# Weighted sums over four streams in a recurrent four-layer kernel: products on DVE replaced by matmuls with diagonal matrices that ACT builds

## The reference

```python
H_res = sinkhorn_log(x_norm @ W_res.T + H_res_base)      # 4x4 per token, 50 iterations
H_pre = softmax(x_norm @ W_pre.T + H_pre_base)           # 4 per token
H_post = softmax(x_norm @ W_post.T + H_post_base)        # 4 per token
H_res = (1.0 - g) * I + g * H_res
x_pre = einsum('btnc,btn->btc', x_streams, H_pre)        # branch input
y = x_pre @ W_branch
x_mixed = einsum('btij,btjc->btic', H_res, x_streams)    # mixture
return (x_mixed + einsum('btc,btn->btnc', y, H_post)).reshape(B, T, nC)
```

## Time and profile before

| | us |
|---|---|
| median of 3 runs | 1445.67 |
| lowest and highest | 1438.63, 1447.93 |
| the profiled execution | 1444.44 |
| its span, first to last instruction | 1442.7 |
| PE, DVE, ACT, POOL busy | 1098.7, 871.4, 578.9, 320.4 |

### The profile page before, as it was taken

How to read it: one execution, slowest core, us unless ns; L and a number is a source line. 1 busy time by engine, 2 the same in 40 slices (tenths; PEclk the granted TensorE clock), 3 DMA queues, 4 the chain that set the end, 5 groups by cost and what they waited for, 6 DMA issues and landing times.

```text
span 1442.7 us, 20140 instructions
## 1 busy us (share of the span) xinstructions
PE 1098.7 (76%) x7480; PEld 446.7 (31%) x7480; DVE 871.4 (60%) x1777; ACT 578.9 (40%) x801; POOL 320.4 (22%) x514
## 2 busy tenths in 40 slices
PE   2889998977788568648437367878788988898887
PEld 1434443433233223314213012312222233333333
DVE  4222221005667589885898887657667587736663
ACT  2433332003554423145114146574445555434452
POOL 1145542017722101011011053700100031111220
PEclk9889999996999678768678588988789999999999
DMA  7322210012100002001101021401012111211100
GB/s 278 118 66 66 69 62 0 0 45 85 46 21 18 7 18 66 12 1 51 33 17 52 24 68 43 131 17 39 17 32 63 51 42 31 70 47 30 52 17 30
DMA packets 54901, 69.74 MB, mean 48 GB/s; under 512 B 9526, under 2 KB 43444, under 8 KB 54800
## 3 DMA queue, kind: packets, MB, share of 16 engines
q1 hardware_dynamic: 50828, 58.58, 12.9%
q0 software_dynamic: 3984, 9.98, 2.3%
HBM read 49.45 MB, written 18.82 MB: 47 GB/s over the span
## 4 chain that ended last, share of the span: by engine, by line
PE 36%; DVE 31%; ACT 5%; issue 4%; SPq 1%; DMA 1%; ACTq 0%; DVEq 0%
DVE w_mx L1404 13%; PE w_banks L669 10%; PE w_po L1319 9%; PE w_banks L1301 4%; PE w_banks L1273 4%; DVE w_region L1891 3%; PE w_banks L1261 2%; ACT w_pr L1347 2%; DVE w_region L1888 2%; DVE w_region L1869 2%; DVE w_region L1886 2%; PE w_banks L1329 2%; PE w_banks L1555 2%; DVE w_region L1884 1%; DVE w_region L1882 1%
## 5 line engine op out<-in xcount | busy, mean ns | idle before, releaser
L1404 DVE TENSOR_REDUCE w_mx<-w_banks 128x2 f32<-128x1024 f32 (+3 forms) x352 | 376.8, 1086 | 195.7 <-PE w_banks L1273 191.4
L1347 ACT ACTIVATE w_pr<-w_banks 128x1024 f32<-128x1024 f32 (+1 forms) x312 | 315.0, 1013 | 429.6 <-PE w_banks L1301 428.3
L1386 POOL TENSOR_SCALAR_AFFINE_SELECT w_pr<-w_pr 128x512 f32<-128x512 f32 (+1 forms) x184 | 104.6, 569 | 561.1 <-ACT w_pr L1347 561.0
L1301 PE MATMUL w_banks<-w_qs,w_ks 49*128 49x512 f16 (+7 forms) x832 | 136.7, 353 | 89.9 <-DVE w_mx L1404 58.8
L1273 PE MATMUL w_banks<-w_ks,w_qs 48*128 48x512 f16 (+7 forms) x832 | 145.0, 361 | 40.5 <-DVE w_mx L1404 23.3
L1319 PE MATMUL w_po<-w_pr,w_vz 128*17 128x512 f32 (+7 forms) x1152 | 154.2, 561 | 12.7 <-ACT w_ou L1369 12.7
L78 PE MATMUL f_pp<-xt,sl_region 128*128 128x512 f16 x672 | 148.9, 382 | 3.5 <-POOL sl_region L508 3.5
L1261 PE MATMUL w_banks<-mask_half,ident_half 64*128 64x128 bf16 (+1 forms) x768 | 67.3, 255 | 37.8 <-DMA w_ks<-stack_scratch 17.1
L482 DVE TENSOR_TENSOR sl_region<-sl_region,f_pp 128x512 f32<-128x512 f32 x28 | 19.2, 687 | 121.1 <-ACT sl_region L497 121.1
L78 PEld LDWEIGHTS f_pp<-xt,sl_region 128*128 128x128 f16 x672 | 65.1, 98 | 84.6 <-issue 5.3
L1301 PEld LDWEIGHTS w_banks<-w_qs,w_ks 49*128 49x128 f16 (+1 forms) x832 | 41.7, 98 | 138.5 <-issue 57.5
(11 more groups left out here) (222 smaller groups left out, 1513.9 us busy)
## 6 DMA issues: line engine op xcount, KB each, us to landing
stack_scratch<-sl_region SPq DMA_DIRECT2D x102, 128.0 KB
w_qs<-stack_scratch SPq DMA_DIRECT2D x96, 96.0 KB, 2.4
sl_region<-in_L_gu SPq DMA_DIRECT2D x14, 512.0 KB
w_stage<-in_L_w POOLq DMA_DIRECT2D x36, 128.0 KB, 2.4
sl_region<-in_L_down SPq DMA_DIRECT2D x14, 256.0 KB
stack_scratch<-p_qk SPq DMA_DIRECT2D x24, 128.0 KB
w_ks<-stack_scratch SPq DMA_DIRECT2D x32, 96.0 KB, 2.6
bw_stage<-in_L_w SPq DMA_DIRECT2D x4, 640.0 KB, 11.8
```

The costliest lines, as they stand in the source:

```text
L1301: mm = pe.matmul(g.banks.pair_at(f)[:, half, at:at + T - q0], g.ks[base:base + self.rows + 1, k_slot, k_place, j * P:(j + 1) * P], g.qs[ba ...
L1347: act.activation(g.probs.at(self.pr_fill[s])[:, :, 0:width], g.banks.pair_at(self.s_fill[s])[:, :, 0:width], ACT.Exp, scale=self.a.scale). ...
L1386: pool.affine_select(out=diagonal, in_=diagonal, compare_op=ALU.is_ge, fill=0.0, base=0, pattern=pattern, channel_multiplier=-1).then_inc( ...
L1404: dve.tensor_reduce(out, g.banks.pair_at(self.m_fill[m])[:, :, 0:heads * keys].rearrange("q h (p k) -> q h p k", k=keys), AX.X, ALU.max).t ...
```

## The change

The sums over the streams are made on PE. A weighted sum of rows by a factor per token is a product with a diagonal matrix of the factors. ACT builds the matrices: `lay` writes the identity times a factor, 128x128 f32 each, into one of two places of `h_dg` (up to five matrices in a place), and waits until PE has used the fill before the last.

- Branch input: for tile i ACT lays four matrices; PE multiplies each stream (as the stationary operand) by its matrix and adds up in PSUM. The result is the sum already transposed, so DVE's products and PE's transposes go. ACT's and DVE's split then reads it, one tick earlier than before.
- Mixture: for each of 16 ticks (tile i, output stream s) ACT lays five matrices, four of H_res and one of H_post; PE makes five matmuls, four of x's streams and one of y, into a pair of banks; ACT takes Silu of two tiles from PSUM. DVE's 64 products and ACT's 16 products of y go.
- `h_om` and `h_xp` are not there any more. The pair of banks is held for eight ticks, the bank of the branch input from its first tile on.
- `small` gets a strand of its own beside layer 0's attention.

```diff
@@ Streams.plan
-        if t == self.pre_at + 5:
-            self.fills["turn"] = self.g.banks.fill(self.lo, 1, (self, t + 2))
+        if t == self.pre_at + 1:
+            self.fills["turn"] = self.g.banks.fill(self.lo, 1, (self, self.pre_at + 6))
+        if t - self.mix_at in (1, 9):
+            pair = (t - self.mix_at) // 8
+            self.fills["mix", pair] = self.g.banks.fill_pair(self.silued, pair + 1, (self, t + 8))
@@ Streams.pe
-            pe.wait_ge(self.pre.sem, self.pre.at + NI * 4)
-            for i in range(NI):
-                mm = pe.transpose(g.banks.at(self.fills["turn"])[:, i * P:(i + 1) * P], g.h_xp[:, i, :], g.ident[:, :])
+            pe.wait_ge(self.laid.sem, self.laid.at + i + 1)
+            for s in range(n):
+                mm = pe.matmul(g.banks.at(self.fills["turn"])[:, i * P:(i + 1) * P], self.xn[:, i, s * P:(s + 1) * P],
+                               g.h_dg[:, i % 2, s, :], start=s == 0, stop=s == n - 1)
+            mm.then_inc(self.used.sem, 1)
...
+        k = t - self.mix_at - 1
+        if 0 <= k < NI * n:
+            i, s = divmod(k, n)
...
+            if k % 8 == 0:
+                g.banks.free(pe, self.fills["mix", i // 2])
+            pe.wait_ge(self.laid.sem, self.laid.at + NI + k + 1)
+            out = g.banks.pair_at(self.fills["mix", i // 2])[:, i % 2, s * P:(s + 1) * P]
+            for j in range(n):
+                pe.matmul(out, g.h_dg[:, k % 2, j, :], self.xn[:, i, j * P:(j + 1) * P], start=j == 0, stop=False)
+            pe.matmul(out, g.h_dg[:, k % 2, n, :], g.h_sq[:, i * P:(i + 1) * P], start=False, stop=True)\
+                .then_inc(self.used.sem, 1)
@@ Streams.act
-            for k in range(n):
-                op = act.activation(g.h_om[:, i % 2, k * P:(k + 1) * P], g.h_sq[:, i * P:(i + 1) * P], ACT.Copy,
-                                    scale=g.h_pp[:, i, n + k:n + k + 1])
-            op.then_inc(self.posted.sem, 1)
+        if 0 <= t - self.mix_at < NI * n:
+            i, s = divmod(t - self.mix_at, n)
+            if t == self.mix_at:
+                act.wait_ge(self.done.sem, self.done.at + 13)
+            self.lay(act, NI + t - self.mix_at, [g.h_mix[:, i, s * n + j:s * n + j + 1] for j in range(n)]
+                     + [g.h_pp[:, i, n + s:n + s + 1]])
+
+    def lay(self, act, q, factors):
+
+        wait_pos(act, self.used.sem, self.used.at + q - 1)
+        for k, factor in enumerate(factors):
+            op = act.activation(self.g.h_dg[:, q % 2, k, :], self.g.ident[:, :], ACT.Copy, scale=factor)
+        op.then_inc(self.laid.sem, 1)
@@ Streams.dve
-            for s in range(n):
-                o = g.h_om[:, i % 2, s * P:(s + 1) * P]
-                if j > 0:
-                    dve.wait_ge(self.mixed.sem, self.mixed.at + i * 16 + (j - 1) * n + s + 1)
-                dve.scalar_tensor_tensor(out=o, in0=self.xn[:, i, j * P:(j + 1) * P],
-                                         scalar=g.h_mix[:, i, s * n + j:s * n + j + 1], in1=o,
-                                         op0=ALU.mult, op1=ALU.add).then_inc(self.mixed.sem, 1)
@@ weave
-        merge([[all_of(small), all_of(a00)], [all_of(split1), lead_of(a01)]], order, emitted, g.banks)
+        merge([[all_of(small)], [all_of(a00)], [all_of(split1), lead_of(a01)]], order, emitted, g.banks)
```

More of the change, by code:

```diff
@@ L1681, with __init__ @@
     N, ITERS, INV_TAU, EPS = 4, 50, 10.0, 1.1920929e-07
-    def __init__(self, g, b, xn, w24, wb, base, gate, norm, weights):
+    def __init__(self, g, b, xn, w24, wb, base, gate, norm, weights, before=None):
         self.g, self.b, self.xn, self.w24, self.wb, self.base, self.gate = g, b, xn, w24, wb, base, gate
-        self.norm, self.weights = norm, weights
+        self.norm, self.weights, self.before = norm, weights, before
         s = g.signals
@@ L1697, in __init__ @@
         self.mix_at = self.gate_at + 3
-        self.ticks = range(self.mix_at + NI * 4 + 1)
+        self.ticks = range(self.mix_at + NI * 4 + 2)
         self.fills = {}
@@ L1721, in pe @@
                 pe.wait_ge(self.norm.lo.sem, self.norm.lo.at + KC)
-                for count, n in self.weights:
-                    pe.wait_ge(count.sem, count.at + n)
+                for count, k in self.weights:
+                    pe.wait_ge(count.sem, count.at + k)
                 g.banks.free(pe, self.fills["logits"])
@@ L1730, in pe @@
                 mm.then_inc(self.made.sem, 1)
-        if t == self.pre_at + 5:
-            g.banks.free(pe, self.fills["turn"])
-            pe.wait_ge(self.pre.sem, self.pre.at + NI * 4)
-            for i in range(NI):
-                mm = pe.transpose(g.banks.at(self.fills["turn"])[:, i * P:(i + 1) * P], g.h_xp[:, i, :], g.ident[:, :])
-            mm.then_inc(self.turned.sem, 1)
-        if t == self.pre_at + 8:
+        i = t - self.pre_at - 1
+        if 0 <= i < NI:
+            if i == 0:
+                g.banks.free(pe, self.fills["turn"])
+            pe.wait_ge(self.laid.sem, self.laid.at + i + 1)
[3 more added lines that the diff above has]
+            mm.then_inc(self.used.sem, 1)
+        if t == self.pre_at + 7:
             g.banks.free(pe, self.fills["branch"])
@@ L1749, in act @@
             if t == 0:
-                wait_pos(act, self.posted.sem, self.posted.at)
+                if self.before is not None:
+                    act.wait_ge(self.before.used.sem, self.before.used.at + self.all_q)
                 act.activation(g.h_gt[:, 0:1], self.gate, ACT.Exp, scale=-1.0).then_inc(self.gate_exped.sem, 1)
@@ L1760, in act @@
             act.activation(g.h_pp[:, :, :], g.h_pp[:, :, :], ACT.Exp).then_inc(self.exped.sem, 1)
-        if t == self.pre_at + 6:
-            act.wait_ge(self.turned.sem, self.turned.at + 1)
+        if 0 <= t - self.pre_at < NI:
+            i = t - self.pre_at
+            if i == 0:
+                act.wait_ge(self.done.sem, self.done.at + 8)
+            self.lay(act, i, [g.h_pp[:, i, s:s + 1] for s in range(n)])
+        if t == self.pre_at + 5:
+            act.wait_ge(self.used.sem, self.used.at + NI)
@@ L1780, in silu @@
+    def lay(self, act, q, factors):
[3 more added lines that the diff above has]
+        op.then_inc(self.laid.sem, 1)
     def silu(self, act, pair):
         g = self.g
-        act.wait_ge(self.mixed.sem, self.mixed.at + 32 * (pair + 1))
-        act.activation(self.xn[:, 2 * pair:2 * pair + 2, :], g.h_om[:, :, :], ACT.Silu).then_inc(self.silued.sem, 1)
+        act.wait_ge(self.used.sem, self.used.at + NI + 8 * (pair + 1))
+        act.activation(self.xn[:, 2 * pair:2 * pair + 2, :], g.banks.pair_at(self.fills["mix", pair]), ACT.Silu)\
+            .then_inc(self.silued.sem, 1)
@@ L1825, in dve @@
                 .then_inc(done.sem, 1)
[L1826 to L1838 removed]
+        elif t == self.pre_at + 6:
             dve.wait_ge(self.hi.sem, self.hi.at + 1)
@@ L2069, in weave @@
     w3 = view(region, 0, (2, KC, 1536), F16)
[L2070 removed]
+    g.h_dg = view(region, 3072, (2, 5, P), F32)
     g.h_xpt, g.h_sq = view(region, 4608, (2, T), F16), view(region, 5120, (D,), F32)
```

44 lines of the change are left out of this document (12 added, 32 removed).

## The result

The changed kernel takes 1460.60 us, median of four runs (1459.37 to 1463.66); the kernel before, beside it on the same chip, 1445.35 (1438.63 to 1447.93). The ratio is 1.0116, with a 95% interval of 1.0078 to 1.0154: some 15 us slower. The profiled execution took 1463.66 us (span 1462.0). Forecast was 1454 with 1442 to 1467. Of eight more runs of this kernel taken later, one took 1975.97 us at a granted clock of 0.631 over its span, in a slow state that the other runs do not show, and it is left out of every comparison.

A forecast was written before the change was run, and what follows sets the result against it. DVE was taken as the fullest engine in the stretch the change touches. Terms -5 + 1 + 11.5 + 1.5 - 1 = +8 us took the profiled 1444.4 to 1452.4, by the median 1453.7, said as 1454 us; range 1442 to 1467.

The forecast's parts named there:

- case A: First mixture: ACT takes DVE's place as the bound, 1454 us, between 1446 and 1463; chance 0.62.
- Start, -5: Start of the woven part: eleven small loads leave the head of SP's queue, -5 us, ends -6.5 and -2.4.
- The eleven issues come back in the middle of layer 0 ... Nothing, or the 3 us once.: Layer 0: eleven load issues push the next loads L1212 by 3 us; costs nothing, or 3 us if a slot were short.
- they fill a slot that is read two groups later: Layer 0: loads pushed by 3 us do no harm, since a group takes some 10 us.
- Branch input 0, +1: Branch input of batch 0: 4.0 us of DVE products go, 5.0 us of ACT products come; +1.0 us on the path.
- sixteen are 5.0 us: Branch input of batch 0: ACT's sixteen products of the identity, from four back to back in 1.26 us.
- The price of an f32 product: PE's 128x128 f32 matmul: 0.25 us at 1.2 GHz, 0.13 at full clock; a tick of five 1.25 or 0.65 us.
- Mixture 0, +11.5: Mixture of batch 0: ACT needs 37.8 us where the window had 27.3, plus 2.5 waits, less 1.5 clock; ends +7, +18.
- Branch input 1, +1.5: Branch input of batch 1: 16 PE matmuls replace 4 transposes, 12 x 0.13 = 1.6 us; +1.5 us, between 0 and 3.
- Mixture 1, -1: Mixture of batch 1: ACT bounds at 29.1 us plus 2 us wait, 31.1 against 32.3; -1 us, between -4 and +5.
- B: Both mixtures: PE's clock comes back to full and the kernel isn't slower, some 1444 us; chance 0.18.
- C: Mixtures: PE and ACT wait for each other in turn, overlap partly lost, +25 us, 1471 us; chance 0.20.

The follow-up runs named there:

- one_pass: The changed kernel with the matmuls by diagonals reading only the upper half (bf16) of each f32: 1446.44 us, ratio 1.0006 to the kernel before.
- dve_lays3: The changed kernel with three of the five diagonals of each mixture tick laid by DVE, not ACT: 1453.85 us, ratio 1.0058 to the kernel before.
- mix0_only: The kernel before with only the mixture of batch 0 moved to PE and ACT: 1455.98 us, ratio 1.0066 to the kernel before.
- again: The changed kernel itself, unedited, measured once more beside the kernel before: median 1456.6 us, ratio 1.0070.

## Why the prediction was right, and where it wasn't

The time lay in the range and on the forecast's side, 6.6 us above the number; case A (ACT bounds the first mixture) is what happened, and one_pass and dve_lays3 show it. That the number came so near is in part luck: two steps were wrong by 6.4 and 2.1 us, one by some 2 the other way, and the same kernel measured again lay at +7.0 us at the 35th marker, below the sum of +8. By its own steps:

- **Start, -5.** Measured -6.0 to -6.4 in nine traces, near the end of -6.5: the 5.1 us of the eleven issues, and 0.8 us of the landing (3.16 us where it was 3.98). POOL came 0.8 us late at its first mask, and not 3 (its splitting ends at 338.3 us, the exponents at 337.46). Right.
- **"The eleven issues come back in the middle of layer 0 ... Nothing, or the 3 us once."** Wrong, and with +6.4 us the largest error of the sum: it took the whole gain of the start back. The step that failed is "they fill a slot that is read two groups later": the slot is read by the maxima, which run ahead of the scores, and PE had nothing else left at 377.7 us, while the loads issued at 378.56. The trace of before has the answer: PE's next L1261 stands 4.5 us behind the start of the loads there, and only 1.2 us behind their landing. The loads were pushed by 3.8 us (3 in the prediction) and landed in 4.4 us in place of 3.0, while the 256 KB rows issued just ahead of them were landing too (the last at 382.80; that these are the reason was not tried). Of this PE lost 4.2 us, and the other 2 behind it, at a granted clock of 0.57.
- **Branch input 0, +1.** Measured +2.9 to +3.2 in six traces. The step that failed is "sixteen are 5.0 us", the diagonals back to back with only the last tile's matmuls behind them: the matmuls of the tiles before do not fit beside ACT's. ACT's timeline shows its last eight diagonals, and then its copy, waiting for PE:

```profile
505.58 1.28 ACT L1813 ACTIVATE w_region<-ident,w_region 128x128 f32<-128x128 f32 x4 [1.06 <-PE w_banks L1746]
507.29 1.28 ACT L1813 ACTIVATE w_region<-ident,w_region 128x128 f32<-128x128 f32 x4 [0.43 <-PE w_banks L1746]
509.81 0.60 ACT L1794 ACTIVATE w_region<-w_banks 128x512 f16<-128x512 f32 x1 [1.25 <-PE w_banks L1746]
```

  PE is the bound there: 6.3 us for 16 products at a clock of 0.60, 0.39 each, where I had 0.25 at the lower level. From the first diagonal to the copy it is 7.7 us, where DVE's products and the transposes took 5.3. "The last tile's matmuls ... cost the same" came true by luck: the clock had risen when they ran, at 508.65 us, and they took 1.1 us as the transposes had at half clock. Of the 3.1, 2.4 us are found so; the rest was not taken apart.
- **The price of an f32 product.** This is what failed at the root of that step: "Ten take 2.50 us ... 0.25 us each". The ten of the earlier trace rows are records, and there are five matmuls (one for each diagonal that DVE makes there); L845 "x2" is one. So a 128x128 product is 0.50 us at 1.2 GHz as a fifth of those 2.50 us, and 0.43 by the starts of the records (0.213 us apart, in the branch input); at 2.4 GHz it is 0.25 and 0.22. The sentence of the Trainium skill that I set aside (FP8 and Floating Point Precision, TensorE Precision Notes: four passes for a true f32 product) agrees with this case: f32 against bf16 is 0.25 to 0.06 us. My estimate of 1.1 us for a tick by that page is what the trace shows too: ten records, 0.11 us apart. PE did not become the bound of the first mixture for that, with 34.6 us busy of 40.6; it came near.
- **Mixture 0, +11.5.** The working held: ACT's 37.8 us were 37.1, the window of 40.3 was 40.6 (39.9 to 40.5 from the first diagonal to the last Silu, in five traces). In the ledger it is +10.4 alone, and 10 to 13 with the branch input's 1.7 taken off. The dearer matmul changed little here, because ACT hid it; it shows as the 3 to 4 us by which one_pass is shorter, and these were in the sum under another name (2.5 us of waits). The 1.5 us for the clock behind the window are not settled: in mix0_only the window grew by 12.7 us and the stage by 10.4, in the changed kernel's first trace nothing came back.
- **Branch input 1, +1.5.** Measured +1.7. That is luck: the 12 x 0.13 us behind it have a product at half its price, so PE got some 3 us of work more, and about half of it was hidden.
- **Mixture 1, -1.** Measured -2.6 from the end of balancing to the end of the last Silu (35.3 us before, 32.8 in the changed kernel, the same in its four traces), and -2.5 to -3.6 at the first marker behind it. The window was right (31.1 forecast, 30.7 from the first diagonal at 822.72 to the end of the Silu at 853.44). What I left out is what stands ahead of it, 1.1 us: before, the last steps of the gate and the first product had to pass two row maxima L1404 on DVE, from the end of balancing at 801.8 to 805.0 us; now the first diagonal waits for one, from 820.7 to 822.7:

```profile
801.75 1.22 DVE L1404 TENSOR_REDUCE w_mx<-w_banks 128x2 f32<-128x1024 f32 x1
803.62 1.22 DVE L1404 TENSOR_REDUCE w_mx<-w_banks 128x2 f32<-128x1024 f32 x1
805.01 1.14 DVE L1869 SCALAR_TENSOR_TENSOR w_region<-sl_region,w_region 128x128 f32<-128x128 f32 x4
```

```profile
821.02 1.23 DVE L1404 TENSOR_REDUCE w_mx<-w_banks 128x2 f32<-128x1024 f32 x1
822.72 7.72 ACT L1813 ACTIVATE w_region<-ident,w_region 128x128 f32<-128x128 f32 x25 [12.54 <-DVE w_region L1882]
```

The sum of +8 against the ledger's +14.2 at the 35th marker: +6.4 (small loads), +2.1 (branch input 0), up to +1.9 (first mixture stage, 14.9 against 13), -1.0 (start), -2.6 (mixture 1 at the 25th marker), -0.6 in balancing. This is the account of one trace. In "again" the sum is +7.0 with the same start, small loads and branch input; the 7.1 us between the two lie in balancing 0 (1.6), in the stage of mixture 0 (3.0) and behind mixture 1 (2.6), and not in the steps above.

Of the rivals, B (the clock comes back and pays) was half right: the clock was 0.88 and 1.00 in the two mixtures against 0.71 and 0.57, and little came of it, as ACT set the pace. C holds for the branch input of batch 0; in the mixtures it is worth the 2 to 4 us that one_pass takes off.

## What to carry to other kernels

Moving sums from a full engine pays only at the place where that engine is full and the receiver is empty: the same edit was worth -2.6 us (up to -3.6 at the next markers) in the mixture where ACT was busy for a fifth of the window, and +10 to +13 us where it was busy for six tenths. Choose per place, by windows. When loads are moved off the head of a queue, look for the place where that queue waits for long and nobody waits for what follows; here three places for the same eleven DMAs (head of the queue, middle of layer 0, behind the second group's loads) were worth 0, 0 and -7 us. And count instructions in the program, not in the trace, before dividing a busy time by a count.
